# A two-block network on one core: the order of each engine's work in block 1 laid out anew

## The reference, cut to what matters

```python
q, k, v = heads(x @ Wq), heads(x @ Wk), heads(x @ Wv)      # 16 heads of 64; 4 memory keys and values in front
dots = einsum('bhid,bhjd->bhij', l2norm(q), l2norm(k)) * 10
dots = einsum('hg,bgij->bhij', W_pre_th, dots)              # mix of heads before the softmax
dots = where(causal, mask, dots)
dots = where(dots < top_k(dots, 64)[0][..., -1:], mask, dots)
attn = einsum('hg,bgij->bhij', W_post_th, softmax(dots))    # mix of heads after it
out = einsum('bhij,bhjd->bhid', attn, v) * head_scale
x = layernorm(x + (out * sigmoid(x @ Wg + bg)) @ Wo)
h = silu(x @ w1) * (x @ w2); h = gelu(h @ h1); h = gelu(h @ h2)
x = layernorm(x + h @ w3)
```

## Time and profile before

| | |
|---|---|
| median of 3 runs | 4013.77 us (4002.79, 4013.77, 4021.79) |
| profiled execution | 4020.4 us, span 4019.1 us |
| mean granted TensorE clock | 0.953 |
| TensorE busy | 3641.7 us, 91% |
| VectorE busy | 3418.9 us, 85% |
| ScalarE busy | 3097.5 us, 77% |
| GpSimd busy | 2068.1 us, 51% |
| DMA | 106.00 MB, mean 26 GB/s |

### The profile page before, as it was taken

The page is one execution under the profiler, slowest core; times in us unless marked ns, Lnnn a source line. Parts: engine busy times, 40 slices in busy tenths (PEclk is TensorE's granted clock), DMA queues, the critical chain, the costliest instruction groups (busy, mean ns, idle before and its releaser), DMA issues.

```text
span 4019.1 us, 78953 instructions
## 1 busy us (share of the span) xinstructions
PE 3641.7 (91%) x19551; PEld 2621.6 (65%) x19551; DVE 3418.9 (85%) x18221; ACT 3097.5 (77%) x10773; POOL 2068.1 (51%) x3991
## 2 busy tenths in 40 slices
PE   5999999986899998999999999999999999999987
PEld 3888888863666666666666666666666666666665
DVE  6888888835998888998999989988888889898894
ACT  5777777755788888888888888888888888888863
POOL 0000000014666667676666766666666766676664
PEclk7999999996999999999999999999999999999998
DMA  3000000001111111111111111111111111111110
GB/s 120 12 11 12 11 12 11 9 9 35 25 27 27 31 30 31 31 27 27 27 28 27 27 27 30 29 26 27 27 30 31 31 30 28 26 27 28 25 25 4
DMA packets 168123, 106.00 MB, mean 26 GB/s; under 512 B 78000, under 2 KB 165104, under 8 KB 166896
## 3 DMA queue, kind: packets, MB, share of 16 engines
q1 hardware_dynamic: 167664, 100.96, 11.7%
HBM read 20.70 MB, written 8.91 MB: 7 GB/s over the span
## 4 chain that ended last, share of the span: by engine, by line
POOL 29%; PE 27%; ACT 25%; issue 10%; DVE 7%; SPq 1%; DMA 1%; POOLq 0%; DVEq 0%; ACTq 0%
POOL below L1849 10%; PE bank L362 6%; POOL T L1859 6%; ACT T L1494 4%; ACT L1463 4%; POOL below L1851 3%; PE bank L330 3%; PE bank L1335 3%; POOL gate L1870 3%; ACT SN L1507 3%; POOL posts L1811 2%; ACT gate L1549 2%; DVE y L895 2%; PE bank L1356 2%; PE bank L431 1%
## 5 line engine op out<-in xcount | busy, mean ns | idle before, releaser
L1714 DVE MATCH_REPLACE8 W<-last,W 128x130 f32<-128x130 f32 (+17 forms) x3456 | 871.5, 259 | 0.0
L1735 DVE MAX8 last<-W 128x8 f32<-128x130 f32 (+17 forms) x3456 | 761.0, 261 | 0.0
L1849 POOL TENSOR_SCALAR below<-T,last 128x260 f32<-128x260 f32 (+8 forms) x576 | 597.7, 1038 | 176.6 <-DVE last L1733 126.2
L1494 ACT ACTIVATE T<-T,peak 128x260 f32<-128x260 f32 (+15 forms) x1024 | 418.1, 422 | 168.0 <-POOL T L1859 159.0
L1811 POOL TENSOR_SCALAR posts<-post,share 128x128 f32<-128x128 f32 x1024 | 376.2, 387 | 246.1 <-DVE share L1644 239.0
L1325 PE MATMUL bank<-T,pre 128*128 128x40 f32 (+15 forms) x1024 | 377.6, 452 | 126.0 <-ACT T L1515 103.5
L1335 PE MATMUL bank<-posts,T 128*128 128x128 f32 (+7 forms) x2048 | 412.2, 307 | 61.2 <-ACT AT L1532 57.8
L885 DVE TENSOR_TENSOR_SCAN hs<-dA,dx 128x256 f32<-128x256 f32 x512 | 349.5, 683 | 134.0 <-issue 100.7
L1507 ACT ACTIVATE SN<-bank,rq 128x260 f32<-128x260 f32 (+1 forms) x1024 | 360.7, 433 | 98.1 <-DMA T<-SN 46.2
L1335 PEld LDWEIGHTS bank<-posts,T 128*128 128x128 f32 (+7 forms) x2048 | 302.5, 182 | 182.7 <-POOL posts L1811 104.2
L521 POOL TENSOR_SCALAR k_sq<-k_sq 128x16 f32<-128x16 f32 x64 | 19.5, 305 | 707.0 <-DVE k_sq L534 572.4
(11 more groups left out here) (242 smaller groups left out, 9503.1 us busy)
## 6 DMA issues: line engine op xcount, KB each, us to landing
T<-SN SPq DMA_DIRECT2D x32, 130.0 KB
x_in<-in_xT SPq DMA_DIRECT2D x32, 128.0 KB, 2.2
x_mid<-x_b SPq DMA_DIRECT2D x32, 128.0 KB, 1.7
xb<-x_mid SPq DMA_DIRECT2D x32, 128.0 KB, 2.1
out_y<-x_d SPq DMA_DIRECT2D x32, 128.0 KB, 3.4
T<-SN SPq DMA_DIRECT2D x32, 126.0 KB
T<-SN SPq DMA_DIRECT2D x32, 122.0 KB
T<-SN SPq DMA_DIRECT2D x32, 118.0 KB
```

The source lines that it names most:

```text
L1494: act.activation(one, one, ACT.Exp, bias=peak[k % 2][:, j:j + 1], accum_out=total[k % 4][:, j:j + 1]).then_inc(e_made, 1)
L1714: dve.match_replace(both[:, s, at:to], best[n], both[:, s, at:to], LOWEST).then_inc(ranked, 1)
L1735: dve.max(best[n], both[:, s, at:to]).then_inc(ranked, 1)
L1849: pool.tensor_scalar(out[:, s, :], x[:, s, :], best[:, 7:8], DROP, ALU.is_lt, ALU.mult).then_inc(marked, 1)
```

## The change

Every constant that places an engine's work on the beats gets a new value. Nothing else is touched: instructions, tiles, semaphores and transfers are the same, and so is VectorE's ranking. The whole diff (its constants):

```diff
-    PE_K = (-19, -19, -2, -1)
-    PE_K_TURN = (-3, 15, 30, 32)
-    PE_Q = (12, 21, 31, 39)
-    PE_Q_SUM = (37, 38, 44, 45)
-    PE_Q_TURN = 54
-    PE_ATTEND = (4, 4, 7, 9)
-    PE_GATES = (44, 46, 49, 51)
-    PE_MIX = (64, 71, 87, 94, 107, 110, 119, 123)
-    PE_OUT = 17
-    PE_VAR1 = 35
-    PE_SPREAD1 = 39
-    PE_W1 = 47
-    PE_W2 = 57
-    PE_H1 = (58, 62, 65, 66)
-    PE_H2 = (76, 81, 89, 91)
-    PE_SCORE0 = (57, 61, 63)
-    PE_W3 = 95
-    PE_SCORE1 = (74, 90, 91, 94, 97, 99, 103, 104)
-    PE_VAR2 = 97
-    PE_SPREAD2 = 105
-    PE_V = (112, 112, 120, 121)
-    PE_PREMIX = [[72, 72, 80, 82, 93, 95, 100, 103], [114, 120, 122, 122, 136, 158, 164, 188]]
-    ACT_K = (3, 5, 21, 24)
-    ACT_K_TURN = (32, 49, 51, 52)
-    ACT_Q = (51, 52, 56, 56)
-    ACT_K_ROOT = (10, 31)
-    ACT_Q_SUM = 60
-    ACT_Q_ROOT = 69
-    ACT_PEAK = (31, 45, 53, 60, 79, 83, 99, 137)
-    ACT_WIDE = (36, 50, 70, 73, 80, 85, 126, 139)
-    ACT_NARROW = (49, 58, 71, 73, 80, 96, 128, 139)
-    ACT_MIX = (74, 81, 85, 117, 130, 131, 138, 146)
-    ACT_SQUARE1 = 51
-    ACT_ROOT1 = 52
-    ACT_GATES = (58, 59, 63, 63)
-    ACT_SILU = (60, 61)
-    ACT_SCORE0 = (70, 72, 72)
-    ACT_H1 = (76, 77)
-    ACT_H2 = (88, 93)
-    ACT_SCORE1 = (83, 85, 89, 96, 107, 113, 117, 124)
-    ACT_SQUARE2 = 104
-    ACT_ROOT2 = 107
-    ACT_V = (135, 137, 138, 141)
-    ACT_PREMIX = [[78, 79, 80, 81, 91, 106, 113, 120], [136, 138, 139, 159, 178, 179, 190, 201]]
-    DVE_SHARE = (40, 66, 80, 84, 108, 111, 120, 135)
-    POOL_GATES = (24, 26, 31, 38)
-    POOL_OPEN = (128, 62, 56, 77)
-    ACT_CTX = (31, 31, 33, 49)
-    DVE_END1 = 56
-    DVE_Q_CLIP = 68
-    DVE_GATED = (69, 69)
-    DVE_END2 = 118
-    POOL_TURN = (-47, -47, -47, 33, 39, 71, 81, 81)
-    POOL_SHARE = (40, 55, 72, 79, 85, 108, 126, 145)
-    POOL_DROP = (22, 38, 47, 60, 78, 84, 100, 136)
-    POOL_ROOT1 = 40
-    POOL_Q_ROOT = 55
-    POOL_ROOT2 = 99
-    POOL_PREMIX = [[83, 84, 85, 85, 90, 124, 128, 129], [130, 136, 156, 158, 166, 184, 203, 209]]
-    ACT_K_SCALE = (13, 34)
-    POOL_K_CLIP = (1, 24)
-    POOL_K_ROOT = (11, 25)
+    PE_K = (-21, -18, 9, 13)
+    PE_K_TURN = (16, 27, 29, 30)
+    PE_Q = (28, 29, 30, 33)
+    PE_Q_SUM = (31, 33, 39, 39)
+    PE_Q_TURN = 58
+    PE_ATTEND = (20, 25, 25, 25)
+    PE_GATES = (37, 44, 47, 57)
+    PE_MIX = (71, 74, 85, 92, 108, 110, 122, 136)
+    PE_OUT = 30
+    PE_VAR1 = 34
+    PE_SPREAD1 = 46
+    PE_W1 = 48
+    PE_W2 = 58
+    PE_H1 = (63, 68, 71, 72)
+    PE_H2 = (78, 80, 82, 88)
+    PE_SCORE0 = (62, 65, 69)
+    PE_W3 = 94
+    PE_SCORE1 = (76, 86, 90, 92, 95, 100, 104, 106)
+    PE_VAR2 = 96
+    PE_SPREAD2 = 107
+    PE_V = (117, 122, 135, 135)
+    PE_PREMIX = [[72, 79, 80, 83, 101, 104, 106, 109], [116, 118, 132, 138, 156, 158, 163, 186]]
+    ACT_K = (-14, -11, 29, 30)
+    ACT_K_TURN = (35, 36, 39, 46)
+    ACT_Q = (37, 43, 48, 50)
+    ACT_K_ROOT = (-4, 34)
+    ACT_Q_SUM = 55
+    ACT_Q_ROOT = 60
+    ACT_PEAK = (31, 40, 49, 62, 72, 81, 85, 127)
+    ACT_WIDE = (38, 44, 62, 65, 78, 91, 115, 133)
+    ACT_NARROW = (40, 61, 65, 68, 81, 91, 116, 134)
+    ACT_MIX = (68, 73, 87, 113, 114, 120, 124, 151)
+    ACT_SQUARE1 = 47
+    ACT_ROOT1 = 50
+    ACT_GATES = (52, 53, 54, 58)
+    ACT_SILU = (55, 55)
+    ACT_SCORE0 = (61, 61, 64)
+    ACT_H1 = (69, 70)
+    ACT_H2 = (82, 90)
+    ACT_SCORE1 = (83, 86, 90, 91, 92, 98, 106, 109)
+    ACT_SQUARE2 = 91
+    ACT_ROOT2 = 95
+    ACT_V = (122, 128, 137, 142)
+    ACT_PREMIX = [[69, 78, 82, 83, 99, 108, 110, 114], [117, 128, 137, 161, 170, 175, 183, 196]]
+    DVE_SHARE = (59, 75, 81, 89, 106, 113, 123, 138)
+    POOL_GATES = (19, 21, 24, 25)
+    POOL_OPEN = (104, 70, 72, 80)
+    ACT_CTX = (31, 35, 36, 42)
+    DVE_END1 = 61
+    DVE_Q_CLIP = 66
+    DVE_GATED = (70, 71)
+    DVE_END2 = 121
+    POOL_TURN = (-62, -62, -62, 11, 21, 50, 71, 66)
+    POOL_SHARE = (34, 62, 64, 65, 78, 87, 106, 138)
+    POOL_DROP = (17, 25, 27, 49, 63, 75, 90, 134)
+    POOL_ROOT1 = 28
+    POOL_Q_ROOT = 48
+    POOL_ROOT2 = 82
+    POOL_PREMIX = [[68, 70, 80, 83, 88, 90, 91, 94], [132, 139, 147, 154, 165, 171, 180, 195]]
+    ACT_K_SCALE = (11, 35)
+    POOL_K_CLIP = (-1, 18)
+    POOL_K_ROOT = (8, 19)
```

## The result

The changed kernel takes 3855.8 us (median of 3851.53, 3852.0, 3859.59 and 3869.06), the kernel before 4017.8 on the same chip: ratio 0.9607, 95% interval 0.9568 to 0.9645. The forecast was 3971 with a range from 3900 to 4046: the direction was right, 43 us were forecast and 162 came. The profiled execution took 3859.6 us (span 3858.3), 160.8 less than before.

The account below looks back on a forecast made before the run. It took a loop through all engines, no single one, to bound the 94.2 us period. Only the tail's 1.4 us counted, other terms nothing: 31 x 1.4 = 43 us gave 3977, 3971 against the median; range 3900 to 4046.

Parts of the forecast that it names:

- Front, TensorE: Period's start: v2 and v3 fill the wait before premix 13, mix 7 avoids the low clock; attention product 1.8 us earlier.
- Front, VectorE: Period's start: share 7 three beats later fills 2.2 of its 2.67 us wait with ranking; no period gain by itself.
- Middle, "partly given back": Attention product to w1: gate product 3 holds the output projection, leaving 0.3 us of the 1.8 there, w1 0.9 earlier.
- Block 0: At w3 and premix 0 of block 0: TensorE waits for the first transfer, leaving 0.4 us of the lead.
- Tail, ScalarE: Three evictions move behind the last SN eviction, which comes 1.4 us earlier and shortens the period by 1.4 us.
- rival B: Block 1's evictions keep step with TensorE's scores, so the transfer hides the gain: no change, 4014; chance 0.18.
- GpSimd in the tail: Posts 5 moves ahead of drop 6; share 6, 3 beats later, covers it: counted nothing, 1.4 us cost if uncovered.
- rival C: GpSimd's queue at the period's end: drop 6 and the ranking end 1.4 us late; slower, 4057; chance 0.20.
- Gate products: GpSimd's products meeting VectorE's two-input work in ranking 2: 1 to 2 us of VectorE could return, counted as nothing.
- Rival A: VectorE becomes the bound and its slack goes through, 3.2 us a period: faster, 3915; chance 0.20.
- What I drew from it for premix 10: Mix 5 ends well before premix 10, which awaits the transfer, so the low clock would move there from mix 7.

Follow-up runs that it names:

- b_warm: The kernel before with eight unread 128x128 matmuls issued ahead of premix 13, where TensorE otherwise waits 2.65 us for ScalarE; ratio to before 0.9872.
- a_front: The changed kernel with v2, v3 and premix 13 moved up again ahead of mix 7's place, the rest new; ratio to before 0.9610.
- b_tail: The kernel before with only premixes 6 and 7 of block 0, their evictions and AT eviction 3 moved behind the last scores and SN evictions; ratio 0.9849.
- a_tail: The changed kernel with premixes 6 and 7 of block 0, their evictions and AT eviction 3 put back in their old places; ratio to before 0.9835.
- b_onein: The kernel before with each two-input gate product on GpSimd replaced by two one-input operations on the same tiles; ratio 0.9997.
- b_out22: The kernel before with TensorE's output projection moved one place later, behind the second query piece (PE_OUT 17 to 22); ratio 0.9916.

## Why the prediction was wrong

1. *Front, TensorE.* The size was near, the mechanism half right: 1.8 us forecast for the attention product, 1.2 measured in the change, 2.1 when the clock alone is repaired (b_warm). What came is the clock; covering the wait shortened nothing (12.9 us at full clock against 12.5), and undoing item 1 in the changed kernel costs 0.2 us (a_front). The single period I took had a front of 14.0 us; the mean was 14.6, since other periods pay 3 us and more for the low level. I should have looked at several.
2. *Front, VectorE.* Right: `share` waits 1.6 us a period, forecast about 2.
3. *Middle, "partly given back".* **This is the step that failed.** I looked for a wait on the way (gate product 3) and let it eat the lead. b_warm shows how little it eats: of 2.1 us at the attention product 1.6 are left at w3, not 0.4, since the wait grows by only 0.4 us: the product comes 1.7 us earlier too. And the new order takes the wait out altogether. In the change w3 comes 3.9 us earlier in its period, 1.2 from the front and 2.7 from the middle up to there, where I had 0.4 in all and put nothing of it into the sum; the middle as a whole is 3.8 us shorter. I read the idle times of the earlier trace rows as fixed; the rows of the middle's windows, 65.07 of 67.60 us busy, would have told me that this stretch is nearly a full queue on TensorE and that its gaps were worth pricing.
4. *Block 0.* Wrong too: TensorE hardly waits for that transfer (0.03 us a period in the middle), so it takes nothing from the lead. Of the 3.9 us, 0.4 are premix 4, which now stands behind w3.
5. *Tail, ScalarE.* The term that made my whole sum. From w3 to the last score the change gains 1.1 us, forecast 1.4, which looks right, but the mechanism is not. In the kernel before, the item alone gives 2.0 us a period (b_tail), and not by ScalarE's freed time: the evictions keep step with the scores, as rival B said, and the gain came over the clock. In the changed kernel it is worth 2.4%, because without it premixes 6 and 7 stall in the middle. The clock falls behind that stall too, but there it costs nothing: a_tail loses 2.7 us a period by it in its tail, and the tail, held by the transfer, is no longer (12.3 us). A period of a_tail, with the stall and what follows it:

```profile
1848.00:1854.40 6.40, 4.31 (x20) 1.98 (x20) 6.38 (x55) 4.26 (x16) 4.98 (x13) 1.00 0.00 1
1854.40:1866.50 12.10, 9.53 (x37) 5.71 (x38) 5.93 (x41) 7.71 (x48) 5.64 (x13) 0.86 0.34 65
```

```profile
1851.92 0.63 PE L1325 MATMUL bank<-T,pre 128*128 128x232 f32 x2 [1.51 <-ACT T L1515]
1853.01 0.71 PE L1325 MATMUL bank<-T,pre 128*128 128x264 f32 x2 [0.46 <-ACT T L1515]
...
1855.38 1.19 PE L431 MATMUL bank<-w_wk,xb 128*128 128x512 f32 x1 [1.02 <-ACT SN L1507]
```

6. *GpSimd in the tail.* Right: GpSimd still waits for the root (107.7 us in 29 waits), no cost of posts 5 is to be seen, and rival C did not come.
7. *Gate products.* Right to count nothing (b_onein).

Rival A's 3915 was nearer, but its reason is not what happened: VectorE is at 87%, and its meetings were worth nothing before. The sum 1.8 + 1.4 without my "given back" would have been 3.2 us and 3915 as well, and nearer by luck in part: the front gave 1.2, and most of what is missing to 5.0 are gaps of the middle that I had not priced.

On the clock: the Trainium skill's "TensorE: Matmul & The Clock Gate", section "HAM oscillation — how this bites in real kernels", ties each wait that is long enough to a fall of the clock behind it. The rows agree only in part: the same 2.65 us wait is followed by the low level in 24 of 28 periods of before and in 7 of 28 of b_out22. What I drew from it for premix 10 came half true. Before, the lower clock started in the front in 24 of 28 periods and in the tail, behind a 1.6 us wait of mix 6, in 14. In the changed kernel none starts in the front any more and 15 of 29 start in the tail, now at premix 10. So the front's loss went away rather than moved: the whole loss was 3.3 us a period before and is 1.1 after (the 0.81 in the quoted texts is too low). Filling the wait at premix 10 gave 0.55%.

What stays open: which places in the new order close the gaps in the middle up to w3. Each part taken alone (b_out22, b_tail, the single engines) made the middle 0.2 us shorter at most, or longer; only the whole was seen to do it. Behind w3 it is item 5, and only together with the rest: without it the changed kernel's middle is as long as before. Nor is it settled why small changes elsewhere (b_tail, b_out22) keep the clock up behind an unchanged wait.

## What to carry to other kernels

Cut a pipelined period at the points where the bounding stretch changes, and read TensorE's idle time in each. In the stretch where it is 96% busy or more, ask first what a gap is worth: in the changed kernel added work cost its length there, but in the kernel before, work taken out turned into idle time. A gap in front of a transfer was worth nothing but what it did to the clock. Before a gain of an edit is booked, check that the granted clock is the same in both traces, since a half-speed stretch of a few microseconds can come or go with any edit and looks like the edit's own effect. A total that fits is no proof of its mechanism: the stretches must fit too. And work out what a matmul costs from the distance between starts (0.112 us here), not from its own duration (0.275).

## What I had not expected of the hardware

Unread matmuls (eight of 128x128, 1.95 us from the first start to the last end) in a wait of TensorE made this kernel 1.3% faster, and the changed one 0.55% faster. One half-speed stretch turned a front of 12.5 us into one of 14.0 to 16.9. And the clock's fall behind one and the same 2.65 us wait is not fixed: 24, 7 and 4 of 28 periods in before, b_out22 and b_tail, and none in b_warm, where the wait was filled.
